# The step order of two causal attentions: a greedy rule inside the kernel against two written-out tables

## What is computed

```python
# layer 0, inside the feed-forward block: 2 x 2048 positions, 16 heads of 16: the "narrow" attention
scores = jnp.einsum('bqhd,bkhd->bhqk', q, k) / math.sqrt(hd)
scores = jnp.where(causal, scores, -1e9)
attn = jnp.einsum('bhqk,bkhd->bqhd', softmax(scores), v) @ Wproj
# layer 1: 16 heads of 32 (real and imaginary halves of 16): the "wide" attention
scores = (einsum(q_r, k_r) + einsum(q_i, k_i)) / jnp.sqrt(jnp.float32(hd))
probs = softmax(where(causal, scores, -inf))
out = concatenate([probs @ v_r, probs @ v_i]) @ Wo
```

## Time and profile before

| | us |
|---|---|
| median of 3 runs (2878.69 to 2886.7) | 2880.25 |
| the profiled execution | 2884.07 |
| its span | 2882.3 |
| TensorE busy (19041 matmuls) | 2675.7 (93%) |
| VectorE busy | 2263.8 (79%) |
| ScalarE busy | 1591.5 (55%) |
| POOL busy | 999.9 (35%) |
| mean granted clock of TensorE | 0.959 of 2.4 GHz |

### The profile page before, as it was taken

How to read it: one execution, slowest core, us unless ns; L and a number is a source line. 1 busy time by engine, 2 the same in 40 slices (tenths; PEclk the granted TensorE clock), 3 DMA queues, 4 the chain that set the end, 5 groups by cost and what they waited for, 6 DMA issues and landing times. The chain is left out here.

```text
span 2882.3 us, 48932 instructions
## 1 busy us (share of the span) xinstructions
PE 2675.7 (93%) x19041; PEld 1238.5 (43%) x19041; DVE 2263.8 (79%) x4752; ACT 1591.5 (55%) x2601; POOL 999.9 (35%) x542
## 2 busy tenths in 40 slices
PE   7998999999999987499998789889999999999999
PEld 4665333333333336366666444323333333333327
DVE  7897899999989947778884676688888888788733
ACT  3542466777666775434442554346665666666561
POOL 1000001100110110321201430257877878778781
PEclk9998899999999998699999999799999999999999
DMA  4232221332132103332311467302020220202203
GB/s 136 88 81 78 49 46 28 64 61 53 28 64 57 28 18 114 77 101 81 121 54 37 151 198 204 104 12 60 12 67 13 69 63 12 67 17 66 70 12 125
DMA packets 142327, 200.93 MB, mean 70 GB/s; under 512 B 14432, under 2 KB 109040, under 8 KB 139136
## 3 DMA queue, kind: packets, MB, share of 16 engines
q1 hardware_dynamic: 131680, 173.21, 21.9%
q0 software_dynamic: 9056, 24.59, 4.1%
q10 hardware_dynamic: 1360, 0.01, 0.0%
HBM read 121.21 MB, written 76.02 MB: 68 GB/s over the span
## 5 line engine op out<-in xcount | busy, mean ns | idle before, releaser
L912 POOL TENSOR_TENSOR at_probs<-at_probs 128x2048 f32<-128x2048 f32 (+3 forms) x205 | 726.4, 3546 | 204.7 <-PE at_acc L1092 111.8
L949 ACT ACTIVATE at_probs<-at_st 128x512 f32<-128x512 f32 (+3 forms) x1280 | 580.4, 550 | 384.2 <-PE at_st L1036 240.9
L394 DVE TENSOR_REDUCE at_part<-at_s 128x1 f32<-128x512 f32 (+3 forms) x1280 | 689.9, 603 | 66.1 <-PE at_s L432 30.4
L369 ACT ACTIVATE at_probs<-at_st 128x1024 f32<-128x1024 f32 (+3 forms) x640 | 541.7, 895 | 278.1 <-PE at_st L451 142.6
L970 DVE TENSOR_REDUCE at_part<-at_s 128x1 f32<-128x512 f32 x768 | 500.3, 681 | 101.0 <-PE at_s L1028 97.8
L511 PE MATMUL at_acc<-at_probs,at_v 128*32 128x512 f32 (+3 forms) x2560 | 307.0, 553 | 8.2 <-ACT at_otile L356 7.8
L964 DVE CUSTOM_DVE_ANT_0 at_s<-at_s,at_later 128x384 f32<-128x384 f32 (+3 forms) x512 | 247.5, 498 | 71.8 <-PE at_s L1028 66.7
L1028 PE MATMUL at_s<-all_k,all_q 96*128 96x512 f16 (+3 forms) x640 | 214.1, 363 | 13.2 <-PEq L43 4.9
L1036 PE MATMUL at_st<-all_q,all_k 98*128 98x512 f16 (+3 forms) x640 | 214.5, 361 | 7.2 <-DMA all_q<-at_strip 5.7
L1036 PE MATMUL at_st<-at_qT,at_kT 98*128 98x512 f16 (+3 forms) x640 | 211.1, 351 | 4.2 <-ACT at_probs L949 2.3
L1028 PE MATMUL at_s<-at_kT,at_qT 96*128 96x512 f16 (+3 forms) x640 | 207.6, 352 | 3.2 <-DVE at_part L970 1.6
(11 more groups left out here) (376 smaller groups left out, 3951.4 us busy)
## 6 DMA issues: line engine op xcount, KB each, us to landing
att<-at_otile SPq DMA_DIRECT2D x64, 256.0 KB, 2.1
lin_w_raw<-in_W SPq DMA_DIRECT2D x16, 1024.0 KB, 5.2
at_v<-v SPq DMA_DIRECT2D x11, 1024.0 KB, 11.2
v<-pr_vt SPq DMA_DIRECT2D x32, 256.0 KB
exp_out<-ex_ot SPq DMA_DIRECT2D x32, 256.0 KB, 2.3
v<-p_vt SPq DMA_DIRECT2D x32, 256.0 KB, 4.2
p_xs<-in_x SPq DMA_DIRECT2D x8, 512.0 KB, 5.3
qhi<-p_parts SPq DMA_DIRECT2D x8, 512.0 KB, 3.7
```

The source lines that it names most:

```text
L369: act.activation(probs[:, quad % RING, heads_down * p:heads_down * (p + 1), off:QB], st_ps[n % st_slots][:, :, off:QB], ACT.Exp, scale=EXP ...
L394: dve.tensor_reduce(part[:, w % 2, qt * HG + h, j:j + 1], s_ps[n % S_SLOTS][:, 0:width], AX.X, ALU.max).then_inc(item_free, 1)
L912: pool.tensor_tensor(total, total, probs[:, slots.slot[quad], :, off:QB], ALU.add).then_inc(add_done, 1)
L949: act.activation(probs[:, slots.slot[quad], h, off:QB], st_ps[n % ST_SLOTS][:, off:QB], ACT.Exp, scale=EXP_SCALE).then_inc(exp_done, 1)
```

## The change

The planning rules go. In their place each stage has a string with one letter for each step of TensorE: `NARROW_ORDER` (2272 letters) and `WIDE_ORDER` (3027 letters). S is the next entry of the score list (a score or a T), P the next key tile (ST), V the next weighing (PV), M the next sum (SM, in the wide string alone). Within each kind the order is unchanged. The other entries of the list are placed by what they follow: M of VectorE behind its unit's last score, EV behind the unit's last PV, A when its key tiles and its set's first weighing are in the list, N 3, 5 and 7 score tiles behind a unit's last sum. The code that turns the list into instructions is unchanged but for the two calls. The diff, cut to its core (the beginnings and ends of the strings are shown):

```diff
+NARROW_ORDER = (
+    "SSSSSSSSSSSSSSSSSSSSSSSSSSSSSSPSSPSSSPSSSSSPSSSSSSSPSSPSSVSSSPSSSSSVPSSSPSSSPPSSSSSSVPSPSSSPSVSS"
...
+    "VPSSSPSPVPSPSSPSPSSPVPSSPSVVPSPVPSSPVPPVPSPVPPVPPPPVVVPPVPPVPPVV"
+)
 def narrow_schedule():
-    while at < len(ahead) or n_pair < len(pairs) or n_quad < len(steps):
-        choice = []
...
-        _, _, kind, start = min(choice)
+    scores = iter(ahead)
+    turned = iter([("ST",) + step + (part,) for step in steps for part in range(parts)])
+    weighed = iter([("PV",) + step for step in steps])
+    body, made = [], 0
+    for kind in NARROW_ORDER:
         if kind == "S":
+            body.append(next(scores))
+            made += 1
+            if made < len(ahead) and ahead[made][0] == "M":
+                body.append(next(scores))
+                made += 1
+        elif kind == "P":
+            body.append(next(turned))
         else:
+            body.append(next(weighed))
+            _, unit, kc = body[-1]
+            if kc == 4 * unit[1] + 3:
+                body.append(("EV", unit))
+    return units, body
+WIDE_ORDER = (
+    "SSSSSSSSSSSSSSSSSSSSSSSSSSSSSSSSSSPSPPSSSSSPSSPSPPSSPPSSPSPSVSPSVSPPSSSSPPSVSVSSPSSPPSPSSPSPPPSS"
...
+    "PSPPSPSSPSSPPPVVPPPSMPPPVVPPPPVPMPPPVMPPPMPPPMPPPMMVVV"
+)
 class WidePlan:
-    S_SLOTS = ST_SLOTS = 3
-    TO_SUMS, FROM_SUMS, SEEN = 97, 145, 202
-    LEAD = 72 * QB
+    FIRST_DIVISION, NEXT_DIVISION = 3, 2
...
     def run(self):
-        emit = {"S": self.score, "ST": self.turn_keys, "PV": self.weigh, "SM": self.sum_up}
-        while self.at < len(self.ahead) or len(self.pv) < len(self.steps) or len(self.total) < len(self.slots.first):
-            ranked, _, kind = min(self.choices())
-            emit[kind](ranked - 150 if kind == "SM" else ranked)
+        emit = {"S": self.score, "P": self.turn_keys, "V": self.weigh, "M": self.sum_up}
+        for kind in WIDE_ORDER:
+            emit[kind]()
         self.divide()
-        return self.units, self.body, (self.pe, self.dve, self.act, self.pool)
+        return self.units, self.body
```

More of the change, by code:

```diff
@@ L62, in narrow_schedule @@
 def narrow_schedule():
-    heads_down, st_slots, s_slots = 2, 2, 3
+    heads_down = 2
     parts = HG // heads_down
     units = [(g, u) for g in range(GROUPS) for u in ((0, 1, 2, 3) if g == 0 else (3, 2, 1, 0) if g == GROUPS - 1 else (2, 0, 3, 1))]
-    place = {unit: n for n, unit in enumerate(units)}
-    ahead, late, count = [], None, {}
+    ahead, late = [], None
     for unit in units:
[L70 to L81, removed]
+        tiles = [("S", unit, qt, h0 + y, j, QB if j < unit[1] else (qt + 1) * P)
+                 for qt in range(4) for h0 in range(0, HG, heads_down) for j in range(unit[1] + 1) for y in range(heads_down)]
+        ahead += tiles[0:4] + ([("T", late)] if late else []) + tiles[4:] + [("M", unit)]
@@ L573, in __init__ @@
-        self.row, self.at, self.made = {}, 0, 0.0
-        self.scored = self.turned_cols = 0
-        self.acc_free = self.sum_free = self.inverse = 0.0
-        self.divisions = []
-        self.body = []
[L579 to L582, removed]
-        if s.role[old] == 0:
-            n, ends = s.set_of[old], self.total
-        else:
-            n, ends = s.add_of[old] - 1, self.add
-        return max(ends[n], self.pv[old]) if n < len(ends) and old < len(self.pv) else None
@@ L636, in add_up @@
                 return
-            ready = max(self.pool, self.exp[HG * quad + HG - 1] + 30,
-                        self.pv[first] + self.SEEN if s.role[quad] == 1 else 0.0)
-            self.add.append(ready + HG * self.width[quad] * 2.11 + 200)
-            self.pool = self.add[-1] + 80
             self.body.append(("A",) + self.steps[quad])
+            self.adds += 1
     def divide(self):
-        over = self.at >= len(self.ahead)
-        while self.divisions and (over or self.divisions[0][2] <= len(self.tile_free)):
-            unit, part, _, end = self.divisions.pop(0)
+        while self.divisions and (self.at >= len(self.ahead) or self.divisions[0][2] <= self.scored):
+            unit, part, _ = self.divisions.pop(0)
@@ L707, in weigh, with sum_up @@
         self.add_up()
-    def sum_up(self, start):
-        n, s = len(self.total), self.slots
-        unit, kc = self.steps[s.first[n]]
+    def sum_up(self):
+        s = self.slots
+        unit, kc = self.steps[s.first[self.summed]]
         self.body.append(("SM", unit, kc))
-        self.summing = True
-        self.pe = start + self.width[s.first[n]] * 4 / 2.4 + 30
-        self.total.append(self.pe)
-        if self.steps[s.last[n]][1] == 4 * unit[1] + 3:
-            at = len(self.tile_free)
-            self.divisions += [(unit, part, at + 3 + 2 * part, self.pe) for part in range(3)]
-            self.sum_free = None
+        if self.steps[s.last[self.summed]][1] == 4 * unit[1] + 3:
+            self.divisions += [(unit, part, self.scored + self.FIRST_DIVISION + part * self.NEXT_DIVISION)
+                               for part in range(3)]
```

268 lines of the change are left out of this document (71 added, 197 removed).

## The result

| | before | after |
|---|---|---|
| median, us | 2879.47 (2874.13 to 2886.70, 4 runs) | 2814.10 (2811.79 to 2814.78, 4 runs) |
| the profiled execution's span, us | 2882.3 | 2810.1 |
| from the first narrow score to the last weighing | 825.6 | 808.0 |
| from the first wide score to the last weighing | 1005.3 | 953.6 |

What follows compares the result with a forecast made beforehand. Wide taken as bound by TensorE; in narrow, VectorE and TensorE wait in turn, VectorE having more work. 6 + 13 + 3 + 4 + 22 + 8 - 5 = 51 us off 2884 gives 2833, less 3.8: 2829 us; range 2787 to 2872.

Steps and rivals of the forecast that it cites:

- Wide, changes: Wide stage, TensorE: changes between weighing/summing and the rest fall from 571 to 511, at 0.105 us each; 6 us off.
- Wide, steady waits: Wide steady groups: weighings stand further behind their quad's last key tile, so waits shrink; 13 us off, bounds 0 and 46.
- Wide, start: Wide group 0: about twice the work between a shift's transpose and its key tile covers the DMA wait; 3 us off.
- Wide, end: End of the wide stage: scores fill places where key tiles in rows wait for ScalarE; 4 us off, bounds 0 and 8.
- Narrow, steady: Narrow stage while scores run: stretches of three or more steps without a score fall from 59 to 18; 22 us off.
- part 7: Last group of each stage: TensorE waits for the shift's DMA before a unit's first key tile; costs 5 us in all.
- Narrow, end: End of the narrow stage, 998 to 1087 us: fewer weighings left after the last score; 8 us off, at most 23.
- Only the countable part: Rival: VectorE sets its own rate and TensorE's order can't help; 16 us off, 2864 us; chance 0.15.
- The search did more: Rival: two thirds of the 136 us of bounds in both stages arrives, 91 us off, 2789 us; chance 0.09.
- Slower by sums: Rival: sums stand too near POOL's adds and hold everything behind them; 2919 us with 20 such sums; chance 0.09.

## Why the prediction was right or wrong

**Wide, changes: right.** 6 us forecast for 60; 0.107 us each measured, 7 to 8 us in the steady groups, where 66 of the changes went. The Trainium skill's sentence that a change of tiling mode drains the engine ("TensorEngine Tiling (Array Packing)", "Key Properties") fits this price; no run here shows that it is a drain.

**Wide, steady waits: the size about right, the reason wrong.** A group takes 115.0 us (690.1 / 6; before, 721.2 / 6 is 120.2), where 117 was forecast. I took 13 us and laid them to weighings that stood too near their exponentials. TensorE's starts show 43.5 us beyond the columns between scores, key tiles and transposes before and 27.9 after: 15.6 us. Entering a weighing was as cheap before as after. The step that failed is the reading of 40.1 us of weight loads "held by ScalarE's exponential" as something on the path; in the same 240 quads it still is 39.9 us. The 7 us that are left are steps done elsewhere: 20 fewer scores, 8 fewer key tiles and 2 fewer sums lie between the 40th and the 280th weighing, 6.8 us of columns. They are no gain of the whole; the start and the end have them.

**Wide, start: too small by 13 us.** I counted idle time behind a DMA (5.7 us) and took half. I didn't ask what else TensorE was doing between a transpose and the first key tile: scores at VectorE's pace with the granted clock at 0.81, visible in the windows. It was the new order's mixing of two units' work that paid there, although the new start holds 6 more scores, 7 more key tiles and 2 more sums. How the 16 us divide between filled waits and clock stays open (about 7 for the clock by the estimate above).

**Wide, end: right** (4.3 for 4), with 14 more scores in it than before.

**Narrow, steady: too large, 5.4 for 22.** The step that failed is the bound of 58 us: VectorE's idle time was taken as room, with TensorE's price of a stretch as the only other thing. But TensorE and ScalarE take 530 us for the 240 quads even with half of VectorE's work gone, and the eviction stood in the way with 8.6 us of late starts in these groups, later 17.4, of which neither the old rule nor my list of parts had an entry. The long stretches did fall from 59 to 18; VectorE's waits fell by 17%, not by the third that was to show it. I said in part 7 that the last group's DMAs would be new waits; the new wait was at ScalarE's program order. The trace of before named it, 6.0 us in 13 pieces, below what I read.

**Narrow, end: about right,** 10.7 for 8, of a part that begins with the 280th weighing and not at 998 us: 18 us after the last score, and ScalarE 68.8 of the last 81 us busy, as said.

**Part 7: right in kind.** TensorE waits for the strip copies in the last groups, 1.6 us in the narrow one and 2.4 in the wide one:

```profile
PE at_st L897 <- DMA at_qT<-at_strip: 2.4, 3, 1.2
```

**The rivals.** "Only the countable part" fell with the ratio, though for the narrow stage alone it was nearly so. "The search did more" was half right, in the wide stage. "Slower by sums" didn't come: in the whole wide stage weight loads of sums waited 6.4 us for POOL; but the kernel with later weighings shows that the mechanism is real and near.

**A version that beats both** is the new tables with the early eviction: 0.9690 and 0.9687 of before on two chips, another 22 us below the kernel after.

## What to carry to other kernels

In a fixed order of steps, the long step that needs no score or key tile (here the weighing) is the breathing space of the engines that empty them: in this order, moving a hundred of them some five steps either way, with the same instructions and the same number of changes, cost 25 and 49 us. Before a search over one engine's order, look at the program order of its partners; one eviction behind an exponential was worth as much as the whole search in that stage. And size a gain by what the second engine needs as well, not by the first one's idle time: halving one operation's work shows that floor in one run.

## What was not expected of the hardware

The granted clock fell to half during scores that came one at a time behind VectorE. Over that part TensorE was called busy for 90.1 of 102.1 us (granted clock 0.81), but less around a fall: 7.1 of the 11 us from 1885 to 1896. Matmuls put into the waits right behind ran at the low level too (0.46 us per 512 columns against 0.22). At a stage's start, where another engine set the pace, 7 us less at the low level saved nothing. The same kernel of before took 2878 us on one chip and 2895 to 2903 on others.
